# A first phase by whole batches of 512 columns in a LoRA and cross-attention kernel

## The chip, the cores and the metric

The kernel runs on one NeuronCore of a Trainium2 chip. The metric is the device time of one execution in microseconds, from the start to the end of the program on that core. In the profile, PE is TensorE (matmuls), DVE is VectorE, ACT is ScalarE, POOL is GpSimd, and SP is SyncE, whose queue only issues transfers here. All data is float32 in DRAM.

## The reference

Two layers over x of 4 batches x 512 tokens x 1024 features, with a context of 4 x 64 vectors:

```python
# layer 0: eight low-rank updates, mixed by a router
w     = softmax(einsum('bsh,nh->bsn', x, router_W) + router_b)        # 8 experts
a_sum = einsum('bsh,arh->bsr', x, ctx_4096)                           # 4 blocks of 64 rows, summed
y     = einsum('bsr,nhr->bsnh', a_sum, lora_B)
h     = nan_to_num(x + 0.5 * einsum('bsn,bsnh->bsh', w, y), nan=0, posinf=1e4, neginf=-1e4)
# layer 1: cross-attention, 32 heads of 32, 64 keys per batch, then layernorm
Q = (h @ Wq.T + bq);  K = (ctx @ Wk.T + bk);  V = (ctx @ Wv.T + bv)
attn = softmax(where(mask, Q K^T / sqrt(32), -inf))
z    = h + (attn V) @ Wo.T + bo
out  = (z - mean) / sqrt(var + 1e-5) * ln_g + ln_b
```

## The kernel before

Every large product is made in three: each float32 operand is split in a high part (rounded to the type float32r, by ACT) and a low part (the rest, by DVE), and `three` (line 499) adds high x high, high x low and low x high in PSUM. The instruction lines are L503, L504 and L505.

The first phase works on units of 256 tokens, two to a batch, eight in all. `UNIT_A` (lines 253 and 254) writes out the order in which every engine's queue goes through a unit: the logits and the low-rank sums ("route", float32 products of 72 columns), transposes of the routed rows ("expand"), eight updates ("u0" to "u7"), each the 128 rows of one chunk of h, and eight query chunks of the *previous* unit ("q0" to "q7"). While unit 0 runs, the query places hold the keys' and values' products instead ("project", KEYS_VALUES), which are float32 products without splitting. Batch 0 is written out, batches 1 to 3 are a hardware loop.

One update goes through the engines so. PE: 12 products into a bank `ps_up`. DVE: `t_sb` = 0.5 x product + x (L745), `pos` and `neg` (L750, L751), `finite` (L752). POOL: `h_t` = pos + neg (L1106). DVE: where finite, t_sb is copied over h_t (L758), which counts `h_ready`. ACT: `act_hi` = high part of h_t (L955). DVE: `act_lo` = low part (L762). PE: `h_rows` transposes h_t for the residual (L533), three chunks behind the updates, and DVE copies it out with the output bias (L770), so that it is stored as `h_rows` in DRAM. Queries are copied from PSUM by ACT (L961) and stored in DRAM whole.

The second phase is attention in 86 steps, one chunk of four heads x 256 tokens a step: scores, softmax, transposes, context, and a part of the output projection, each engine a few steps behind the other (`step` of each engine). It loads queries, keys and values from DRAM and splits them there (q: L1021 on ACT, L1119 on POOL; keys: L1004, L820; values: L1015, L829). The projection begins in step 14. The queries of the last unit stand in steps 0 to 7, and the output weights are loaded, split and put in the place of the query weights during steps 4 to 13 (`WO_SPLITS`).

SP's queue is one order for loads and stores; weights pass a ring of four `stage` tiles, and `load_weight(n)` (line 350) waits until the low part of weight n - 4 is made (`stage_lo`). All engines' queues run in the order written; an instruction that waits on a semaphore holds all behind it.

Of the kernel before, what the change touches and what calls it, by code (L numbers as in the profile page):

```python
# [13 lines left out]
P = 128  # L28
NB = 4
TOK = 512  # L30
H = 1024
KC = H // P
U = 256
UB = TOK // U
TU = U // P
CB = UB * KC
# [10 lines left out]
FAR = 3.0e38  # L47
ACT_HEADS = 4
EXPS = ACT_HEADS + 1
EPS = 1e-5  # L50
WARM = 28

REGION_3 = max(2 * KC * U + 2 * RC * U + 6 * U + 2 * U // 4, 4 * TU * HPC * V + 8 * U + 8 * U + 4 * U + 2 * KC * V)
REGION_4 = max(4 * U + 2 * NR * R + KC * LOG + 8 * P * TU + H + NR + TU * (R + 2 * NR + 3) + 64, 2 * H)


def live(i, n, per):


    return n < per and (not isinstance(i, int) or i * per + n >= 0)  # L60


def wait(eng, sem, value):

    if not isinstance(value, int) or value > 0:
        eng.wait_ge(sem, value)


def xattn_kernel(nc, xT, ctxT, mask, BT, rWT, rb, WqT, bq, WkT, bk, WvT, bv, WoT, bo, ln_g, ln_b, out):
    x_v = xT.rearrange("b (k p) t -> b p k t", p=P)  # L70
    w_v = {n: w.rearrange("(k p) n -> p k n", p=P) for n, w in
           (("q", WqT), ("k", WkT), ("v", WvT), ("o", WoT), ("B", BT))}
    ctx_v = ctxT.rearrange("(k p) v -> p k v", p=P)

    hn_d = nc.dram_tensor("h_rows", (NB, UB, U, H), F32, kind="Internal").ap()
    q_d = nc.dram_tensor("q_cols", (NB, UB, KC // 2, P, 2 * U), F32, kind="Internal").ap()

    k_d = nc.dram_tensor("keys", (NB, P, KC, V), F32, kind="Internal").ap()
    v_d = nc.dram_tensor("values", (NB * V, H), F32, kind="Internal").ap()
    k_chunks = k_d.rearrange("b p c v -> c p b v")  # L80
    v_heads = v_d.rearrange("(b v) (c s d) -> b s v c d", v=V, s=2, d=HD)
    hn_pairs = hn_d.rearrange("b u (t p) (g n) -> b u g p t n", p=P, n=2 * P)
    hn_tiles = hn_d.rearrange("b u (t p) n -> (b u t) p n", p=P)
    out_v = out.rearrange("b (t p) n -> (b t) p n", p=P)

    with ExitStack() as ctx:
        def sb(name, shape, dt=F32, stack=ctx):
            return stack.enter_context(nc.sbuf_tensor(name, shape, dt))
# [3 lines left out]

        ident = sb("ident", [P, P])
        bq_c = sb("bq_c", [P, KC])
        bk_c = sb("bk_c", [P, KC])
        bv_c = sb("bv_c", [P, KC])
        eps_c = sb("eps_c", [P, 1])
        mask_i = sb("mask_i", [P, NB * V], I32)
# [3 lines left out]

        act_hi = [sb("act_hi0", [P, KC, U], F32R)]
        act_lo = [sb("act_lo0", [P, KC, U], F32R)]
        with ExitStack() as s:
            ctx_t = sb("ctx_t", [P, KC, NB * V], F32, s)
        act_hi.append(sb("act_hi1", [P, KC, U], F32R))
        act_lo.append(sb("act_lo1", [P, KC, U], F32R))  # L110
# [12 lines left out]

        with ExitStack() as s:
            b_hi = sb("b_hi", [P, RC, H], F32R, s)
            b_lo = sb("b_lo", [P, RC, H], F32R, s)
        kbd_hi = sb("kbd_hi", [P, KC, HPC * V], F32R)
        kbd_lo = sb("kbd_lo", [P, KC, HPC * V], F32R)
        vbd_hi = sb("vbd_hi", [P, KC, 2, P], F32R)
        vbd_lo = sb("vbd_lo", [P, KC, 2, P], F32R)  # L130

        region3 = ExitStack()
        x_sb = [sb(f"x_sb{u}", [P, KC, U], F32, region3) for u in range(2)]
        u_hi = sb("u_hi", [P, RC, U], F32R, region3)
        u_lo = sb("u_lo", [P, RC, U], F32R, region3)
        t_sb = [sb(f"t_sb{k}", [P, U], F32, region3) for k in range(2)]
        pos = [sb(f"pos{k}", [P, U], F32, region3) for k in range(2)]
        neg = [sb(f"neg{k}", [P, U], F32, region3) for k in range(2)]
        finite = [sb(f"finite{k}", [P, U], U8, region3) for k in range(2)]
        region3.close()  # L140
        region3 = ExitStack()
        s_sb = [sb(f"s_sb{k}", [P, TU * HPC, V], F32, region3) for k in range(4)]
        p_hi = [sb(f"p_hi{k}", [P, 2, U], F32R, region3) for k in range(2)]
        p_lo = [sb(f"p_lo{k}", [P, 2, U], F32R, region3) for k in range(2)]
        q_hi = [sb(f"q_hi{k}", [P, U], F32R, region3) for k in range(4)]
        q_lo = [sb(f"q_lo{k}", [P, U], F32R, region3) for k in range(4)]
        q_raw = [sb(f"q_raw{k}", [P, 2, U], F32, region3) for k in range(2)]
        k_b = sb("k_b", [P, KC, V], F32, region3)
        v_b = sb("v_b", [P, KC, 2, HD], F32, region3)
        region3.close()  # L150
        sb("region3", [P, REGION_3], F32)

        region4 = ExitStack()
        h_t = [sb(f"h_t{k}", [P, U], F32, region4) for k in range(4)]
        u_sb = [sb(f"u_sb{k}", [P, NR, R], F32, region4) for k in range(2)]
        a_rhs = sb("a_rhs", [P, KC, LOG], F32, region4)
        hn_sb = [sb(f"hn_sb{k}", [P, TU, 2 * P], F32, region4) for k in range(2)]
        q_sb = [sb(f"q_sb{k}", [P, 2, U], F32, region4) for k in range(2)]
        bo_b = sb("bo_b", [P, H], F32, region4)
        rb_b = sb("rb_b", [P, NR], F32, region4)  # L160
        a_sb = sb("a_sb", [P, TU, R], F32, region4)
        lg = sb("lg", [P, TU, NR], F32, region4)
        lg_max = sb("lg_max", [P, TU], F32, region4)
        lg_sum = sb("lg_sum", [P, TU], F32, region4)
        lg_inv = sb("lg_inv", [P, TU], F32, region4)
        w_sb = sb("w_sb", [P, TU, NR], F32, region4)
        region4.close()
        with ExitStack() as s:
            g_b = sb("g_b", [P, H], F32, s)
            lb_b = sb("lb_b", [P, H], F32, s)  # L170
        sb("region4", [P, REGION_4], F32)

        with ExitStack() as s:
            stage = [sb(f"stage{k}", [P, H], F32, s) for k in range(4)]
        z_sb = [sb(f"z_sb{k}", [P, H]) for k in range(4)]
        k_sb = [sb(f"k_sb{k}", [P, NB * V]) for k in range(2)]
        v_sb = sb("v_sb", [P, H // 2])
# [3 lines left out]
        mask_b = sb("mask_b", [P, V])  # L181
# [10 lines left out]
        ps_al = ps[:, 0, 0:TU * LOG].rearrange("p (t n) -> p t n", t=TU)  # L192
        ps_u = [ps[:, 1, :], ps[:, 2, :]]
        ps_up = [ps[:, 3, 0:U], ps[:, 4, 0:U]]
        ps_hn = [ps[:, 5, 0:U], ps[:, 2, 0:U]]
        ps_q = [ps[:, 6, 0:U], ps[:, 7, 0:U]]

        ps_kv = [ps[:, 6, :], ps[:, 7, :]]
        ps_s = [ps[:, 0, :], ps[:, 1, :]]
        ps_t = [ps[:, 2, :].rearrange("p (g n) -> p g n", g=2), ps[:, 3, :].rearrange("p (g n) -> p g n", g=2)]  # L200
        ps_v = [ps[:, 4, 0:U], ps[:, 5, 0:U]]
        ps_o = [ps[:, 6, :], ps[:, 7, :]]


        ident_set, ident_ready = sem("ident_set"), sem("ident_ready")
        warm_set = sem("warm_set")
        small_in, ctx_in, router_in = sem("small_in"), sem("ctx_in"), sem("router_in")
        wk_in, wv_in = [sem(f"wk_in{g}") for g in range(KC // 2)], [sem(f"wv_in{k}") for k in range(2)]
        k_stored, v_stored = [sem(f"k_stored{k}") for k in range(2)], sem("v_stored")
        stage_in = [sem(f"stage_in{k}") for k in range(4)]  # L210
        stage_hi, stage_lo = sem("stage_hi"), sem("stage_lo")
        x_in = [sem(f"x_in{u}") for u in range(2)]
        mask_step, a_step = sem("mask_step"), sem("a_step")
        k_mm, k_out, v_mm, v_out = sem("k_mm"), sem("k_out"), sem("v_mm"), sem("v_out")
# [982 lines left out]
```

## Time and profile before

| | |
|---|---|
| median of three executions | 739.31 us (738.87 to 739.56) |
| profiled execution | 738.63 us, span of its instructions 736.8 us |
| PE busy | 698.5 us, 95% |
| DVE, ACT, POOL busy | 507.0, 323.3, 307.8 us |
| mean granted TensorE clock | 0.985 |
| moved by DMA | 76.83 MB, mean 104 GB/s |

The times of single instructions come from one profiled execution. A matmul's end is modelled and overlaps the next one's start, so that the distance from start to start is what a product costs in a row of products, not its duration. The clock is 1.00 at full speed and 0.50 at half.

### The profile page before, as it was taken

To read this page: it belongs to the slowest core of one execution; us is meant where nothing else is said; L and a number is where in the kernel's file an instruction comes from. 1 tells how busy PE (TensorE), PEld (TensorE's weight loads), DVE (VectorE), ACT (ScalarE), POOL (GpSimd) and SP (SyncE) were. 2 spreads that over 40 slices of the span, in tenths; PEclk is the share of its full clock that TensorE was granted. 3 is DMA by queue.
4 is the path that set the end of the run, shared out by engine and by line. 5 is a ranking of instruction groups with operands and counts; after the bars stand their busy time and mean duration, and the time that the engine had idled before them with its cause. 6 is when DMAs were issued, how large, how long until landed. Compare 5 with 4: busy or idle time off the path is not lost.

```text
span 736.8 us, 14456 instructions
## 1 busy us (share of the span) xinstructions
PE 698.5 (95%) x4764; PEld 638.7 (87%) x4764; DVE 507.0 (69%) x1170; ACT 323.3 (44%) x1061; POOL 307.8 (42%) x343
## 2 busy tenths in 40 slices
PE   9999999999999999999988879999998999999993
PEld 7885699999999999999978768888887888888882
DVE  2547347364745647374667898999999988998733
ACT  0412221212121222112126897777776868777511
POOL 1011022221212212221234685478667876787644
PEclk9999999999999999999999989999999999999997
DMA  8984212513130312211141462013312242222311
GB/s 280 391 294 159 85 58 75 199 44 130 44 114 28 114 57 80 77 43 71 43 115 58 141 188 88 34 51 117 102 44 87 86 117 85 86 85 72 115 58 57
DMA packets 57012, 76.83 MB, mean 104 GB/s; under 512 B 17025, under 2 KB 38657, under 8 KB 56961
## 3 DMA queue, kind: packets, MB, share of 16 engines
q1 hardware_dynamic: 56960, 76.21, 31.0%
q8 instruction: 24, 0.39, 0.2%
q14 instruction: 28, 0.22, 0.1%
HBM read 48.94 MB, written 27.26 MB: 103 GB/s over the span
## 4 chain that ended last, share of the span: by engine, by line
PE 72%; DVE 15%; issue 5%; ACT 5%; DMA 2%; POOL 0%; DVEq 0%; SPq 0%; ACTq 0%
PE ps L503 19%; PE ps L505 19%; PE ps L504 19%; PE ps L606 4%; PE ps L514 3%; PE ps L593 2%; DVE kbd_lo L820 2%; DVE s_sb L842 2%; PE ps L635 2%; PE ps L533 2%; DVE p_lo L859 2%; DVE vbd_lo L829 1%; ACT s_sb L1029 1%; PE ps L568 1%; DMA keys<-k_sb 1%
## 5 line engine op out<-in xcount | busy, mean ns | idle before, releaser
L503 PE MATMUL ps<-act_hi,w_hi 128*128 128x256 f32 x512 | 149.6, 292 | 0.6 <-issue 0.6
L505 PE MATMUL ps<-act_hi,w_lo 128*128 128x256 f32 x512 | 146.2, 286 | 0.0
L504 PE MATMUL ps<-act_lo,w_hi 128*128 128x256 f32 x512 | 146.1, 285 | 0.0
L1106 POOL TENSOR_TENSOR h_t<-pos,neg 128x256 f32<-128x256 f32 x64 | 48.3, 754 | 233.1 <-DVE neg L751 233.1
L503 PE MATMUL ps<-w_hi,act_hi 128*128 128x512 f32 x256 | 105.3, 411 | 4.1 <-DVE act_lo L864 4.1
L955 ACT ACTIVATE act_hi<-h_t 128x256 fp32r<-128x256 f32 x64 | 26.7, 417 | 174.7 <-DVE h_t L758 174.7
L505 PE MATMUL ps<-w_hi,act_lo 128*128 128x512 f32 x256 | 100.4, 392 | 0.0
L504 PE MATMUL ps<-w_lo,act_hi 128*128 128x512 f32 x256 | 100.2, 391 | 0.0
L503 PEld LDWEIGHTS ps<-act_hi,w_hi 128*128 128x128 f32 x512 | 99.4, 194 | 0.8 <-issue 0.8
L1029 ACT ACTIVATE s_sb<-s_sb,s_min 128x64 f32<-128x64 f32 x256 | 85.8, 339 | 31.8 <-DVE s_min L847 31.2
L504 PEld LDWEIGHTS ps<-act_lo,w_hi 128*128 128x128 f32 x512 | 99.4, 194 | 0.0
L505 PEld LDWEIGHTS ps<-act_hi,w_lo 128*128 128x128 f32 x512 | 99.3, 194 | 0.0
L745 DVE SCALAR_TENSOR_TENSOR t_sb<-ps,x_sb 128x256 f32<-128x256 f32 x64 | 26.9, 420 | 81.1 <-PE ps L505 81.0
L1124 POOL TENSOR_TENSOR s_sb<-s_sb,s_inv 128x512 f32<-128x512 f32 x64 | 73.7, 1152 | 16.5 <-DVE s_inv L855 16.4
L503 PE MATMUL ps<-u_hi,b_hi 128*128 128x256 f32 x256 | 74.7, 292 | 0.6 <-DVE u_lo L735 0.6
L505 PE MATMUL ps<-u_hi,b_lo 128*128 128x256 f32 x256 | 72.4, 283 | 0.0
L504 PE MATMUL ps<-u_lo,b_hi 128*128 128x256 f32 x256 | 72.4, 283 | 0.0
L1119 POOL TENSOR_TENSOR q_lo<-q_raw,q_hi 128x256 fp32r<-128x256 f32 x64 | 49.1, 768 | 48.9 <-ACT q_hi L1021 48.8
L503 PEld LDWEIGHTS ps<-w_hi,act_hi 128*128 128x128 f32 x256 | 48.5, 189 | 13.0 <-DVE act_lo L864 4.8
L505 PEld LDWEIGHTS ps<-w_hi,act_lo 128*128 128x128 f32 x256 | 48.2, 188 | 10.8
L961 ACT ACTIVATE q_sb<-ps,bq_c 128x256 f32<-128x256 f32 x64 | 30.0, 469 | 61.0 <-PE ps L505 60.4
L504 PEld LDWEIGHTS ps<-w_lo,act_hi 128*128 128x128 f32 x256 | 48.5, 189 | 8.4
(105 smaller groups left out, 1731.1 us busy)
## 6 DMA issues: line engine op xcount, KB each, us to landing
x_sb<-xT SPq DMA_DIRECT2D x8, 1024.0 KB, 6.0
h_rows<-hn_sb SPq DMA_DIRECT2D x32, 256.0 KB, 2.2
q_cols<-q_sb SPq DMA_DIRECT2D x32, 256.0 KB, 2.1
q_raw<-q_cols SPq DMA_DIRECT2D x32, 256.0 KB, 3.2
z_sb<-h_rows SPq DMA_DIRECT2D x16, 512.0 KB, 3.5
out<-z_sb SPq DMA_DIRECT2D x16, 512.0 KB, 2.9
wk_raw<-WkT SPq DMA_DIRECT2D x8, 512.0 KB, 8.4
wv_raw<-WvT SPq DMA_DIRECT2D x2, 2048.0 KB, 11.4
```

What stands on the lines that cost most here:

```text
L503: pe.matmul(dst, lh, rh, start=(first and j == 0), stop=False)
L504: pe.matmul(dst, lh, rl, start=False, stop=False)
L505: mm = pe.matmul(dst, ll, rh, start=False, stop=(last and j == n - 1))
L514: mm = pe.matmul(ps_al[:, t, :], x_sb[p][:, k, t * P:(t + 1) * P], a_rhs[:, k, :], start=(k == 0), stop=(k == KC - 1))
L606: mm = pe.matmul(ps_kv[n % 2], ctx_t[:, k, t * P:(t + 1) * P], wv_raw[k // HK][:, k % HK, half * (H // 2):(half + 1) * (H // 2)], start=(k ...
L745: dve.scalar_tensor_tensor(t_sb[c % 2][:], ps_up[c % 2], LORA_SCALE, x_sb[u][:, c, :], ALU.mult, ALU.add).then_inc(t_ready, 1)
L955: act.activation(act_hi[m // KC][:, m % KC, :], h_t[m % 4][:], ACT.Copy).then_inc(hhi_done, 1)
L961: act.activation(q_sb[c // 2 % 2][:, c % 2, :], ps_q[c % 2], ACT.Identity, bias=bq_c[:, c:c + 1]).then_inc(q_copied, 1)
L1029: act.activation(s_sb[m % 4][:, h, :], s_sb[m % 4][:, h, :], ACT.Exp, bias=s_min[m % 2][:, h:h + 1], scale=-1.0, accum_out=s_sum[m % 2][:, ...
L1106: pool.tensor_tensor(h_t[m % 4][:], pos[m % 2][:], neg[m % 2][:], ALU.add).then_inc(sign_ready, 1)
L1119: pool.tensor_tensor(q_lo[m % 4][:], q_raw[m % KC // 2 % 2][:, m % 2, :], q_hi[m % 4][:], ALU.subtract).then_inc(qlo_done, 1)
L1124: pool.tensor_tensor(s_sb[m % 4][:], s_sb[m % 4][:], s_inv[m % 2][:].unsqueeze(2).to_broadcast([P, TU * HPC, V]), ALU.mult).then_inc(p_rea ...
```

## The change

The first phase works on whole batches of 512 tokens. Query, update, key and value products all have 512 columns. The order of all engines is written by two functions, without hardware loops. Keys and values are split products as well (context rows stationary, weight rows moving), accumulated over the eight weight rows in four PSUM banks `ps_q`, and so are the queries: a "query" block is one k of the sum for four chunks, 12 products. Queries, keys, values and output weights are split in the first phase and both parts are kept in DRAM, so that the second phase only loads them. Keys are turned by PE ("turn") before they are stored. The transposes of h stand one chunk behind the updates (three before). The update's sum is made in place in `x_sb`, and `h_t` has three tiles of 512 columns. The last 12 query blocks stand in steps 0 to 11 of the second phase. The core of the diff:

```diff
+SEQ = ([("K", k) for k in range(5)] + [("B", k) for k in range(RC)] + [("K", k) for k in range(5, KC)]
+       + [("V", k) for k in range(KC)] + [("Q", k) for k in (0, 1, 3, 4, 5, 6, 7, 2)])
+def first_phase():
+    def up(i, c):
+        return ([("rows", i, c - 1)] if c else []) + [("update", i, c)]
+    out = [("context_in", 0)] + split("K", 0) + [("context_in", 1)] + split("K", 1) + [("keys", 0)] + split("K", 2)
+    out += [("adapter",), ("keys", 1)] + split("K", 3) + [("keys", 2)] + split("K", 4) + [("keys", 3), ("route", 0)]
+    out += split("B", 0, 1) + [("keys", 4)] + split("B", 2, 3) + split("K", 5) + [("keys", 5)] + split("K", 6)
+    out += [("expand", 0, 0), ("keys", 6)] + split("K", 7) + [("expand", 0, 1), ("keys", 7), ("keys_out",)]
+    out += up(0, 0) + split("V", 0) + [("values", 0)] + split("V", 1) + [("mask",), ("values", 1)] + split("V", 2) + up(0, 1)
+    out += [("values", 2), ("turn", 0), ("turn", 1)] + split("V", 3) + [("values", 3)] + split("V", 4) + up(0, 2)
+    out += [("values", 4), ("turn", 2), ("turn", 3)] + split("V", 5) + up(0, 3) + [("values", 5)] + split("V", 6)
+    out += [("values", 6)] + split("V", 7) + up(0, 4) + split("Q", 0) + [("values", 7), ("values_out",)] + split("Q", 1)
+    for i in range(NB):
+        ks = (0, 1, 3, 4, 5, 6, 7, 2) if i == 0 else range(KC)
+        for n, k in enumerate(ks):
+            out += query(i, 0, k)
+            if i == 0 and n < 6:
+                out += split("Q", ks[n + 2])
+            if n in (0, 1):
+                out += up(i, 5 + n)
+            if n == (2 if i == 0 else 3):
+                out += up(i, 7)
+                if i == NB - 1:
+                    return out
+            if n == 4:
+                out += [("rows", i, 7), ("flush", i)]
+            if i in (1, 2) and n >= 4:
+                out += [("output_weight", 8 * (i - 1) + 2 * (n - 4) + h) for h in range(2)]
+        out += [("query_out", i, 0), ("route", i + 1)]
+        for k in range(KC):
+            out += query(i, 1, k)
+            if k in (1, 2):
+                out += [("expand", i + 1, k - 1)]
+            if k == 7:
+                out += [("query_out", i, 1)]
+            if k >= 3:
+                out += up(i + 1, k - 3)
@@ the queue of SP @@
+            def load_weight(n):
+                what, k = SEQ[n]
+                wait(sp, stage_lo, n - 3)
+                sp.dma_start(stage[n % 4][:], w_v[what][k]).then_inc(stage_in[n % 4], 16)
+            def output_weight(n):
...
+                sp.wait_ge(wolo_done, n + 1)
+                for l in range(2):
+                    sp.dma_start(o_d[l, n // 2, :, n % 2 * HALF:(n % 2 + 1) * HALF],
+                                 wo_sb[:, l, :].bitcast(F32)).then_inc(wo_stored, 16)
+                if n + 2 < 2 * KC:
+                    load_raw(n + 2)
+                if n == 2 * KC - 1:
+                    sp.wait_ge(wo_stored, 32 * 2 * KC)
@@ the queue of PE @@
+            def h_rows(i, c):
+                m = KC * i + c
+                pe.wait_ge(h_ready, m + 1)
+                wait(pe, hn_copied, m)
+                for t in range(TT):
+                    mm = pe.transpose(ps_hn[:, t * P:(t + 1) * P], h_t[m % 3][:, t * P:(t + 1) * P], ident[:])
+                mm.then_inc(hn_mm, 1)
...
+            def query(i, g, k):
...
+                if g == 0:
+                    pe.wait_ge(hlo_done, KC * i + k + 1)
+                for j in range(4):
+                    if first:
+                        if i == 0 and g == 0:
+                            pe.wait_ge(kvlo_done, 4 + j + 1)
+                        else:
+                            pe.wait_ge(q_copied, KC * i + 4 * g + j - 3)
+                    cols = slice((4 * g + j) * P, (4 * g + j + 1) * P)
+                    mm = three(ps_q[j], [(w_hi[:, k, cols], w_lo[:, k, cols], act_hi[:, k, :], act_lo[:, k, :])],
+                               first=first, last=last)
+                    if last:
+                        mm.then_inc(q_mm, 1)
+                if not last:
+                    mm.then_inc(block_mm, 1)
@@ the queue of DVE @@
+            def update(i, c):
+                m = KC * i + c
+                t_c = x_sb[:, c, :]
+                dve.wait_ge(up_mm, m + 1)
+                dve.scalar_tensor_tensor(t_c, ps_up[c % 2], LORA_SCALE, t_c, ALU.mult, ALU.add).then_inc(t_ready, 1)
+                wait(dve, sign_ready, m - 1)
+                wait(dve, h_ready, m - 1)
+                dve.wait_ge(t_ready, m + 1)
+                dve.tensor_scalar(pos[m % 2][:], t_c, 0.0, 1e4, ALU.is_gt, ALU.mult).then_inc(sign_step, 1)
+                dve.tensor_scalar(neg[m % 2][:], t_c, 0.0, -1e4, ALU.is_lt, ALU.mult).then_inc(sign_step, 1)
+                if c:
+                    h_low(m - 1)
+                dve.tensor_scalar(finite[m % 2][:], t_c, 0.0, 0.0, ALU.mult, ALU.is_equal).then_inc(f_ready, 1)
+                if c:
+                    copy_h_rows(m - 1)
+                dve.wait_ge(f_ready, m + 1)
+                dve.wait_ge(sign_ready, m + 1)
+                dve.copy_predicated(h_t[m % 3][:], finite[m % 2][:], t_c).then_inc(h_ready, 1)
@@ the queue of ACT @@
+            def update(i, c):
+                m = KC * i + c
+                act.wait_ge(h_ready, m + 1)
+                if i >= 1 and c < KC - 1:
+                    act.wait_ge(block_mm, 14 * (i - 1) + 7 + c + 1)
+                if i >= 1 and c == KC - 1:
+                    act.wait_ge(q_mm, KC * i)
+                act.activation(act_hi[:, c, :], h_t[m % 3][:], ACT.Copy).then_inc(hhi_done, 1)
...
+            def output_weight(n):
+                act.wait_ge(wo_raw_in[n % 2], 16 * (n // 2 + 1))
+                wait(act, wo_stored, 32 * n)
+                act.activation(wo_sb[:, 0, :], wo_raw[n % 2][:], ACT.Copy).then_inc(wohi_done, 1)
```

Left out of the diff here: the tiles' new addresses, `turn` and `values_out` (ACT makes the high part of a bank into one of two tiles `kv_sb`, DVE the low part, SP stores both; a tile is used again when its stores have landed), the loads of q, k, v parts in the second phase, and the steps of attention, whose products and order stay.

## Rows read from the trace of the kernel before

**Rows 1.** The page, busy time by engine: us, share of the span, instructions.
```profile
PE 698.5 (95%) x4764; PEld 638.7 (87%) x4764; DVE 507.0 (69%) x1170; ACT 323.3 (44%) x1061; POOL 307.8 (42%) x343
```
**Rows 2.** Stages on all engines: length, busy us (count) by engine, clock, DMA share, GB/s.
```profile
85.07:374.80 289.73, 286.17 (x2410) 284.61 (x2408) 167.55 (x456) 59.91 (x134) 57.16 (x71) 1.00 0.23 80
374.80:439.74 64.94, 50.72 (x365) 48.21 (x363) 51.85 (x96) 48.13 (x172) 38.11 (x39) 0.91 0.43 131
439.74:703.00 263.26, 256.77 (x1529) 226.62 (x1528) 235.81 (x506) 192.28 (x718) 190.36 (x208) 1.00 0.26 84
```
**Rows 3.** PE in order of time: start, us, line; transposes in a unit, and an update's end.
```profile
137.30 1.04 PE L525 MATMUL ps<-ident,u_sb 128*128 128x128 f32 x8
138.09 0.36 PE L503 MATMUL ps<-act_hi,w_hi 128*128 128x256 f32 x1
...
148.01 0.28 PE L504 MATMUL ps<-u_lo,b_hi 128*128 128x256 f32 x1
148.13 0.28 PE L505 MATMUL ps<-u_hi,b_lo 128*128 128x256 f32 x1
```
**Rows 4.** PE in order of time, output projection in the second phase, 512 columns.
```profile
442.54 0.39 PE L503 MATMUL ps<-w_hi,act_hi 128*128 128x512 f32 x1
442.76 0.39 PE L504 MATMUL ps<-w_lo,act_hi 128*128 128x512 f32 x1
```
**Rows 5.** The chain that ended last: start, us, what.
```profile
11.12 3.76 PE ps L514 x32
...
64.43 20.62 PE ps L606 x48
...
126.81 3.53 PE ps L514 x32
```
**Rows 6.** DVE in order of time, one update of 256 columns.
```profile
148.45 0.42 DVE L745 SCALAR_TENSOR_TENSOR t_sb<-ps,x_sb 128x256 f32<-128x256 f32 x1 [2.80 <-PE ps L505]
148.91 0.30 DVE L750 TENSOR_SCALAR pos<-t_sb 128x256 f32<-128x256 f32 x1
149.12 0.28 DVE L751 TENSOR_SCALAR neg<-t_sb 128x256 f32<-128x256 f32 x1
...
149.52 0.42 DVE L762 TENSOR_TENSOR act_lo<-h_t,act_hi 128x256 fp32r<-128x256 f32 x1
149.86 0.98 DVE L758 COPY_PREDICATED h_t<-finite,t_sb 128x256 f32<-128x256 uint8 x1
```
**Rows 7.** Groups by line on DVE, ACT and POOL: busy us, mean ns, idle before.
```profile
L842 DVE SCALAR_TENSOR_TENSOR s_sb<-ps,mask_b 128x512 f32<-128x512 f32 x64 | 43.7, 683 | 14.9 <-PE ps L505 13.6 <-PE ps L635 0.8
L691 DVE TENSOR_TENSOR w_lo<-stage,w_hi 128x1024 fp32r<-128x1024 f32 x16 | 19.4, 1244 | 1.5 <-ACT w_hi L939 1.5
...
L939 ACT ACTIVATE w_hi<-stage 128x1024 fp32r<-128x1024 f32 x16 | 16.2, 1047 | 15.3 <-PE ps L606 15.3
...
L1124 POOL TENSOR_TENSOR s_sb<-s_sb,s_inv 128x512 f32<-128x512 f32 x64 | 73.7, 1152 | 16.5 <-DVE s_inv L855 16.4
L1130 POOL TENSOR_TENSOR s_sb<-s_sb,s_min 128x256 f32<-128x256 f32 x64 | 41.9, 654 | 29.4 <-DVE s_min L847 29.2
```
**Rows 8.** POOL in order of time, the same update and the next.
```profile
149.62 0.91 POOL L1106 TENSOR_TENSOR h_t<-pos,neg 128x256 f32<-128x256 f32 x1 [3.41 <-DVE neg L751]
153.80 0.73 POOL L1106 TENSOR_TENSOR h_t<-pos,neg 128x256 f32<-128x256 f32 x1 [3.27 <-DVE neg L751]
```
**Rows 9.** DVE in order of time at the start: the adapter's first sum, the router's last step.
```profile
6.40 0.69 DVE L685 TENSOR_TENSOR a_rhs<-ctx_t 128x512 f32<-128x512 f32 x1 [5.00 <-DMA ctx_t<-ctxT]
...
16.47 0.17 DVE L726 TENSOR_TENSOR w_sb<-lg,lg_inv 128x16 f32<-128x16 f32 x1
```
**Rows 10.** Tiles stage and q_sb: transfers to landing, and SP's issue of the stores.
```profile
DMA to landing us min/median/max: 3.4/7.7/12.7
...
L378 SPq DMA_DIRECT2D q_cols<-q_sb x32: 332/344/1006, 96.6 to 417.4; - x32
...
DMA to landing us min/median/max: 2.0/2.1/3.9
```

More of the change, by code:

```diff
@@ L47 @@
 FAR = 3.0e38
+EPS = 1e-5
+WARM = 22
+U = 256
+TU = U // P
+UNITS = NB * TOK // U
+CHUNKS = UNITS * KC
+TILES = NB * TOK // P
+GROUPS = 2 * TILES
+STEPS = CHUNKS + 22
 ACT_HEADS = 4
 EXPS = ACT_HEADS + 1
[L50 to L60, printed above, removed]
+BASE = 6144
@@ new lines, in second_phase @@
+def second_phase():
+    last = NB - 1
+    left = {0: [("query", last, 0, 4), ("rows", last, 7), ("flush", last)], 1: [("query", last, 0, 5)],
+            2: [("query", last, 0, 6)], 3: [("query", last, 0, 7), ("query_out", last, 0)]}
+    for n in range(8):
+        pair, k = n // 4, n % 4
+        left[4 + n] = [("pair", pair, 2 * k), ("pair", pair, 2 * k + 1)] + ([("pair_out", pair)] if k == 3 else [])
+    out = []
+    for s in range(STEPS):
+        out += left.get(s, []) + [("step", s)]
+    return out
@@ L171, in xattn_kernel @@
[L171 to L177, printed above, removed]
+        rb_b = sb("rb_b", [P, NR])
+        a_sb = sb("a_sb", [P, TT, R])
+        lg = sb("lg", [P, TT, NR])
+        lg_max = sb("lg_max", [P, TT])
+        lg_sum = sb("lg_sum", [P, TT])
@@ L506, in three, with project @@
                 return mm
-            def a_and_logits(i, p):
-                wait(pe, x_in[p], 16 * (i + 1))
-                wait(pe, route, 7 * (UB * i + p))
-                for t in range(TU):
+            pe.wait_ge(warm_set, 1)
+            for n in range(WARM):
+                pe.matmul(ps_up[0], act_hi[:, 0, 0:P], act_hi[:, 0, :], start=True, stop=True)
+            def project(what, k):
+                s = slot_of(what, k)
+                pe.wait_ge(stage_lo, PLACE[what, k] + 1)
+                for g in range(4):
+                    t, cols = g // 2, slice(g % 2 * HALF, (g % 2 + 1) * HALF)
+                    if what == "V" and k == 0:
+                        pe.wait_ge(k_copied, g + 1)
+                    rows = slice(t * P, (t + 1) * P)
+                    mm = three(ps_q[g], [(ctx_hi[:, k, rows], ctx_lo[:, k, rows], w_hi[:, s, cols], w_lo[:, s, cols])],
+                               first=(k == 0), last=(k == KC - 1))
+                return mm
@@ L674, in _, with step @@
-            run_phase_b(pe, step, lambda m: query(NB - 1, KC * (UB - 1) + m))
+            def step(s):
+                if live(s - 2, CHUNKS):
+                    scores(s - 2)
+                if live(s - 5, CHUNKS):
+                    p_transposed(s - 5)
+                o, part = output_group(s)
+                if live(o, GROUPS):
+                    projection(o, part)
+                if live(s - 6, CHUNKS):
+                    context(s - 6)
+            run({"keys": keys, "values": values, "turn": turn, "route": a_and_logits, "expand": expand, "update": update,
+                 "rows": h_rows, "query": query, "pair": pair, "step": step})
@@ L1102, in signs @@
-            def signs(i, m):
-                wait(pool, sign_step, 2 * (i * CB + m) + 2)
-                wait(pool, hn_mm, i * CB + m - 3)
-                wait(pool, hlo_done, i * CB + m - 3)
-                pool.tensor_tensor(h_t[m % 4][:], pos[m % 2][:], neg[m % 2][:], ALU.add).then_inc(sign_ready, 1)
-            run_phase_a(pool, {"route": lambda i, p: None, "expand": expand, "update": signs,
-                               "query": lambda i, m: None, "flush": lambda i, p: None,
-                               "rows": lambda i, p: None, "project": lambda n: None})
@@ new lines, in signs, with update, zero @@
+            def signs(m):
+                pool.wait_ge(sign_step, 2 * m + 2)
+                wait(pool, hn_mm, m - 2)
+                wait(pool, hlo_done, m - 2)
+                pool.tensor_tensor(h_t[m % 3][:], pos[m % 2][:], neg[m % 2][:], ALU.add).then_inc(sign_ready, 1)
+            def update(i, c):
+                signs(KC * i + c)
+            def zero():
+                pool.wait_ge(up_mm, ALL)
+                for z in (kbd[0], kbd[1], vbd[0], vbd[1]):
+                    pool.memset(z[:].bitcast(F32), 0.0).then_inc(zeroed, 1)
```

1362 lines of the change are left out of this document (621 added, 741 removed).

## The prediction

> **What bounds the kernel now.** I read the busy line first: TensorE (PE) 698.5 of 736.8 us, VectorE (DVE) 507, ScalarE (ACT) 323 [rows 1]. A busy share is an average, so the table by stages comes next [rows 2]. From 85.07 to 374.80 us (seven units of 256 tokens, 41.4 us each) PE is busy 286.2 of 289.7 us: the order in which PE's queue is written decides, and there is almost no wait in it. From 374.80 to 439.74 (attention starting up beside the last eight queries) PE is busy 50.7 of 64.9 us at a mean clock of 0.91. From 439.74 to 703.00 PE has 256.8 of 263.3 us. So time is won only by taking work from PE, and anything that makes PE wait is lost in full. The profiled execution took 738.63 us, 1.8 us around its span of 736.8, and 0.7 us below the median of 739.31.
>
> **What wider matmuls are worth.** Start to start, a 256-column product takes 0.12 us [rows 3] and a 512-column one 0.228 (0.22 to 0.23, [rows 4]); two narrow ones cost 0.240. Queries and updates have 64 x 24 + 64 x 12 = 2304 narrow products, which become 1152 wide ones: 1152 x 0.012 = 14 us. Keys and values: 24 full-precision products of 512 columns took 20.62 us [rows 5], 0.86 each; split, three take 0.68, and there are 64 in keys and values together: 64 x 0.18 = 11 us. Attention needs no splitting of q, k, v any more; its steps are then bound by PE (below). That is the gain, about 35 us with the better cover at the handover. It is what the waits have to be set against. The loops written out cost nothing that a row shows, since PE has no gap at a loop's turn in [rows 2]; the zeroing of four tiles on POOL lies under the last query blocks.
>
> **The chain of one update, 512 wide.** Call S the start of an update's last product. Now DVE starts 0.32 us after it (148.13 to 148.45, [rows 3, 6]); at 512 columns the product lasts 0.11 longer [rows 4]: 0.43. The scaled sum takes 0.42 at 256 [rows 6] and an operation like it 0.68 at 512 [rows 7], 0.26 more. Pos to neg is 0.21 at 256 [rows 6]; these compare at about twice the pace, so 0.13 more, 0.34. neg ends at about 1.91, and GpSimd (POOL) starts 0.08 later, at 1.99. Its sum is 0.73 at 256 [rows 8]; the pair 0.654 and 1.152 [rows 7] gives 0.5 more for 256 columns: 1.23. But DVE's low part of the previous chunk now stands between neg and finite, starts 0.1 us ahead of POOL and takes 0.69; a short version of this is in the trace: DVE at 149.52, POOL at 149.62, and POOL takes 0.91, not 0.73 [rows 6, 8]. So POOL ends near 3.67, and the predicated copy (a clear pass from SBUF takes 0.42 at 256 [rows 6], so 0.7 here) gives h_ready at 4.5.
> PE transposes a chunk's rows right before the *next* update (three chunks later before). Where one query block (12 x 0.228 = 2.74) stands between two updates, PE is at the transposes at S + 2.97 and waits 1.54 us. Places, from the written order: up 0 to 4 of the next batch, four; rows 4, 5 and 7 of a batch, three; batch 0 has two. 2 + 4 + 3 + 4 + 3 + 4 + 3 = 23, one of them after the handover. 23 x 1.54 = 35 us. Bounds: 1.04 each if POOL isn't delayed (24 us); if finite must wait for POOL as well, all that follows it comes after 3.67 and the wait is 2.4 (55 us).
> The predicated copy that began while POOL ran (149.86) took 0.98 [rows 6]. No row has finite beside POOL, and I take it as free, like the PSUM reads. The Trainium skill (SBUF - State Buffer, section "SBUF: two separate sides") says that a DVE instruction in a two-port mode, or with two SBUF inputs, and a GpSimd one lock each other out for the whole instruction; that row agrees; if finite counts as two-port, the sum would be by 20 us and more higher, the second rival below.
>
> **The start, walked.** Context lands at 6.4 [rows 9]. ACT's high part (1.05 for 1024 columns) and DVE's low part (1.24, [rows 7]) of half the context and of K0 follow: first keys at 9.9. PE work from there to the first query: 192 products of keys and values 43.8, one route 2 x 3.53 = 7.1 [rows 5], 16 + 16 transposes 3.5 (8 take 0.79, [rows 3], and the product behind them 0.08 more), five updates 13.7, rows 1.8: 69.8. Waits in it:
> - K5 follows four B parts in a ring of four stages, and B0 is split behind the router (1.65 us, from 14.88 [rows 5] to 16.6 [rows 9]). B0's two parts follow, and K5 is asked for 3.4 us after the route ends at 27.9; landing 3.4 to 12.7, median 7.7 [rows 10], I take 5 with the queue empty; two parts 2.3. Ready at 38.3, PE free at 30.7: 7.6.
> - ACT's act_hi of an update waits for that update's h_ready, and the V parts and turns stand behind it in ACT's queue. After update 0 (DVE copies four key banks first): V0 ready at 58.4, PE free at 51: 7.4. After update 1: the two turns, one PSUM bank, and V3: 5.9. After update 2, the turns: 3.1. After update 3, V6: 4.5. Update 4, Q0, then four value groups through two buffers, each store landing in 2.1 [rows 10]: 8.0.
> Together 36.5 us (25 to 50, by the landing and by the chain). The transfers themselves are no bound: their share is 0.23 in phase one now [rows 2], and halves of q, k, v and the output weights add less than that again. First query at 9.9 + 69.8 + 36.5 = 116.2.
>
> **The output weights.** In batches 1 and 2 eight halves pass one tile wo_sb: ACT 0.6 (1.05 for twice the columns, [rows 7]), DVE 0.69, two stores issued by SyncE at 0.35 each, the second landed 2.1 later [rows 10], then ACT goes on: 4.2 with the handshakes (3.7 if the minimum landing of 2.0 and overlap hold). ACT's copy of the query group stands behind all eight, and PE needs its bank after the route. PE is there at S + 20.2 (S of update 7; queries 4 to 7 with one wait, then 7.1). ACT gets there at S + 41.3 in batch 1 (the first raw half is only asked for behind the flush), S + 36.5 in batch 2. 21 + 16 = 37 us (28 to 45).
>
> **Sum.** Rest of phase one: 52 query blocks 142.5, 27 updates 74.0, rows 11.9, three routes 21.2, expands 5.2: 254.8. With 22 waits 33.9, a Q part late in batch 0 by 1.4, and 37: phase one ends at 116.2 + 254.8 + 33.9 + 1.4 + 37 = 443.3. Handover to the first projection: 12 query blocks now cover it, four steps with 2.74 each, scores and one wait 14.4, then ten steps at 4.4 on the mean, 44 (PE's work in one with a query block is 4.6, in one without 1.9; now the fourteen take 4.6 each): 58.4 (64.9 now, [rows 2]). SyncE's 32 extra loads a batch (0.34 each at least, [rows 10]) are asked for four steps ahead and are hidden; without that cover 3 us a batch. The 56 full steps take 263.3 now, 4.70 each; PE's work in one is 24 products, 4.64 us, so 4 us go, and 297.1 - 4 = 293 remain to the end. 443.3 + 58.4 + 293 = 794.7. Eight waits of 3 us and more let the clock fall: the handover lost 0.09 x 64.9 = 5.8 us of clock in four falls [rows 2]; eight cost some 9.5 (0 to 18). Span 804, device time **806 us**, 9% slower.
>
> **Rivals.**
> - *Finite waits for POOL too.* For: it has the quick pace of pos and neg, and both of its ends are in SBUF; against: DVE's small tensor_scalars weren't delayed. 20 us at the transposes, 5 at the start, 4 clock: 835. Chance 0.28.
> - *Store round trips are cheap or overlapped*, so ACT is with the query group in time: 806 - 37 - 3 = 766. For: 15 us of cover; against: eight round trips in series. Chance 0.1.
> - *ACT's queue doesn't hold PE* (the other side): start waits and output weights are all queue order on ACT and the stage ring, 73.5 us and 9.5 of clock. Without them 806 - 83 = 723, faster. It decides where less than 15 us of them stay. For: ACT is only 44% busy [rows 1]; against: each wait is on a semaphore that the same queue reaches later. Chance 0.08.
> - *The transposes don't wait, beside it* (the change does only what it says): 690. Chance 0.03.
> - *Worse*: repeated waits keep the clock at half: above 850. Chance 0.06.
> - Forecast, 780 to 825: 0.45.
>
> **Numbers.** Range 760 to 845: it takes in the cheap round trips and the first rival, and leaves out 0.08 + 0.03 + 0.06 and a little. Within 0.2% (what these runs can tell from nothing) 0.01; faster 0.1; slower 0.89.
>
> **What would show it.** Profile after: PE's busy share well under 90%; waits "ps <- h_t" of 1.5 us on the row transposes, 20-odd times; two waits of 15 to 21 us before a query group in the middle; phase one ending near 443; no waits in attention above those of now. It is wrong if h_ready comes within 3 us of S, if the landing of small stores is hidden, or if K5 and V0 arrive before PE wants them.

## The result

The changed kernel takes 877.62 us (median of four executions, 875.64 to 880.06) against 739.25 for the kernel before: ratio 1.1894 (95% interval 1.1864 to 1.1924). The direction was forecast, the size was not: 806 was predicted, and 877.62 lies above the range's upper end of 845. The profiled execution has a span of 876.3 us and a mean clock of 0.907.

The page of the changed kernel, its busy time and its clock in 40 slices, answers to [rows 1]:

```profile
PE 718.9 (82%) x3622; PEld 605.9 (69%) x3622; DVE 497.9 (57%) x914; ACT 295.4 (34%) x891; POOL 258.7 (30%) x249
...
PEclk9887877899899689899698898899999999999998
```

PE has 1142 fewer matmuls than before and is nevertheless busy for 20 us longer. The line of the clock shows why: digits of 6 to 8 stand all over the first 26 slices. The table by stages, with the columns of [rows 2]; the borders are the first query product, the last update's last product and the first product of the output projection:

```profile
0.00:127.70 127.70, 89.68 (x386) 72.68 (x387) 64.12 (x87) 32.41 (x40) 13.79 (x16) 0.86 0.53 168
127.70:510.80 383.10, 291.47 (x1296) 236.06 (x1297) 168.83 (x265) 55.62 (x90) 54.53 (x38) 0.86 0.33 111
510.80:587.70 76.90, 60.55 (x317) 51.92 (x315) 41.71 (x80) 34.62 (x134) 27.32 (x28) 0.90 0.66 233
587.70:876.30 288.60, 277.24 (x1628) 245.23 (x1626) 223.23 (x484) 172.70 (x627) 163.04 (x167) 0.98 0.37 116
```

PE stands still for 38.0, 91.6, 16.4 and 11.4 us in the four. I take half of PE's busy time at half clock (1.2 of 2.4 GHz) as what the clock costs. Summed over the trace's records it is 11.5, 33.2, 6.4 and 1.0 us, 52.1 in all; all such sums below are made in this way. What PE waited for, in total, times and longest:

```profile
PE ps L599 <- DVE h_t L810: 48.3, 23, 2.6
PE ps L516 <- DVE q_sb L819: 41.4, 3, 22.1
PE ps L516 <- DVE w_lo L722: 25.4, 6, 7.2
PE ps L516 <- DMA qb<-q_cols: 10.9, 3, 5.4
PE ps L516 <- DVE kv_sb L739: 9.0, 2, 5.8
PE ps L553 <- DVE kv_sb L734: 7.4, 2, 3.7
```

L599 is the transposes of h, L516 the first product of `three`. The 23 waits are the 23 that were counted from the order, but they are not 1.54 us each: nineteen are 2.2, three 1.3 and one 2.6, 2.1 on the mean. One of them on PE; the last product of an update starts at S = 228.31:

```profile
228.31 0.40 PE L518 MATMUL ps<-u_hi,b_lo 128*128 128x512 f32 x1
...
231.06 0.39 PE L518 MATMUL ps<-act_hi,w_lo 128*128 128x512 f32 x1
233.64 0.66 PE L599 MATMUL ps<-ident,h_t 128*128 128x128 f32 x4 [2.19 <-DVE h_t L810]
...
234.94 0.63 PE L516 MATMUL ps<-u_hi,b_hi 128*128 128x512 f32 x1
235.37 0.63 PE L517 MATMUL ps<-u_lo,b_hi 128*128 128x512 f32 x1
```

After the wait the products stand 0.43 us apart, no longer 0.23. The same update on DVE, and then on POOL:

```profile
228.75 0.69 DVE L797 SCALAR_TENSOR_TENSOR x_sb<-ps,x_sb 128x512 f32<-128x512 f32 x1 [5.09 <-PE ps L518]
229.57 0.43 DVE L801 TENSOR_SCALAR pos<-x_sb 128x512 f32<-128x512 f32 x1
229.91 0.42 DVE L802 TENSOR_SCALAR neg<-x_sb 128x512 f32<-128x512 f32 x1
230.25 0.69 DVE L784 TENSOR_TENSOR act_lo<-h_t,act_hi 128x512 fp32r<-128x512 f32 x1
230.85 1.50 DVE L805 TENSOR_SCALAR finite<-x_sb 128x512 uint8<-128x512 f32 x1
232.28 0.68 DVE L790 TENSOR_TENSOR hn_sb<-ps,bo_b 128x512 f32<-128x512 f32 x1
232.88 0.71 DVE L810 COPY_PREDICATED h_t<-finite,x_sb 128x512 f32<-128x512 uint8 x1
```
```profile
230.41 1.66 POOL L1076 TENSOR_TENSOR h_t<-pos,neg 128x512 f32<-128x512 f32 x1 [8.28 <-DVE neg L802]
```

`finite` reads what `pos` reads, and takes 1.50 us where that takes 0.43 (its output is uint8, but it takes 0.43 as well where POOL is idle, as the last but one experiment shows): it ends at 232.35, just after POOL (232.07). So the copy of the previous rows and the predicated copy stand behind POOL's sum, and h is ready at S + 5.28, not S + 4.5.

### The profile page after: what moved, and what is told of

Same layout as the page of the kernel before. It is cut to its first block, busy times and chain, and to the rows that moved or that the text cites. A ratio compares the mean times of both kernels' runs of the same rounds, so it can differ in the third digit from the quotient of the medians.

```text
span 876.3 us, 10740 instructions
## 1 busy us (share of the span) xinstructions
PE 718.9 (82%) x3622; PEld 605.9 (69%) x3622; DVE 497.9 (57%) x914; ACT 295.4 (34%) x891; POOL 258.7 (30%) x249
## 4 chain that ended last, share of the span: by engine, by line
PE 61%; DVE 17%; DMA 8%; issue 6%; SPq 3%; ACT 3%; POOL 2%; DVEq 0%; ACTq 0%; POOLq 0%
PE ps L516 18%; PE ps L517 18%; PE ps L518 18%; DMA output_weights<-wo_sb 4%; DVE finite L805 3%; PE ps L658 3%; PE ps L599 2%; DVE h_t L810 2%; DVE x_sb L797 2%; DVE hn_sb L790 2%; DVE act_lo L784 2%; PE ps L567 2%; DMA qb<-q_cols 2%; DVE wo_sb L832 1%; DVE neg L802 1%
## 5 line engine op out<-in xcount | busy, mean ns | idle before, releaser
L516 PE MATMUL ps<-act_hi,w_hi 128*128 128x512 f32 x256 | 106.2, 415 | 52.4 <-DVE q_sb L819 41.4
L1076 POOL TENSOR_TENSOR h_t<-pos,neg 128x512 f32<-128x512 f32 x32 | 51.9, 1622 | 290.6 <-DVE neg L802 290.6
L516 PE MATMUL ps<-wo_hi,cx_hi 128*128 128x512 f32 x256 | 105.1, 411 | 0.0
L517 PE MATMUL ps<-act_lo,w_hi 128*128 128x512 f32 x256 | 104.0, 406 | 0.0
L518 PE MATMUL ps<-act_hi,w_lo 128*128 128x512 f32 x256 | 103.6, 405 | 0.0
L517 PE MATMUL ps<-wo_lo,cx_hi 128*128 128x512 f32 x256 | 100.6, 393 | 0.0
L518 PE MATMUL ps<-wo_hi,cx_lo 128*128 128x512 f32 x256 | 100.5, 393 | 0.0
L516 PEld LDWEIGHTS ps<-act_hi,w_hi 128*128 128x128 f32 x256 | 50.9, 199 | 64.9 <-DVE q_sb L819 41.9
L797 DVE SCALAR_TENSOR_TENSOR x_sb<-ps,x_sb 128x512 f32<-128x512 f32 x32 | 22.1, 692 | 125.3 <-PE ps L518 125.3
L599 PE MATMUL ps<-ident,h_t 128*128 128x128 f32 x128 | 23.7, 315 | 48.3 <-DVE h_t L810 48.3
L516 PE MATMUL ps<-u_hi,b_hi 128*128 128x512 f32 x128 | 62.5, 489 | 0.0
L517 PE MATMUL ps<-u_lo,b_hi 128*128 128x512 f32 x128 | 59.0, 461 | 0.0
L518 PE MATMUL ps<-u_hi,b_lo 128*128 128x512 f32 x128 | 58.2, 455 | 0.0
L599 PEld LDWEIGHTS ps<-ident,h_t 128*128 128x128 f32 x128 | 16.3, 157 | 59.4 <-DVE h_t L810 58.0
```

The source lines that it names most:

```text
L516: pe.matmul(dst, lh, rh, start=(first and j == 0), stop=False)
L517: pe.matmul(dst, lh, rl, start=False, stop=False)
L518: mm = pe.matmul(dst, ll, rh, start=False, stop=(last and j == n - 1))
L599: mm = pe.transpose(ps_hn[:, t * P:(t + 1) * P], h_t[m % 3][:, t * P:(t + 1) * P], ident[:])
L797: dve.scalar_tensor_tensor(t_c, ps_up[c % 2], LORA_SCALE, t_c, ALU.mult, ALU.add).then_inc(t_ready, 1)
L1076: pool.tensor_tensor(h_t[m % 3][:], pos[m % 2][:], neg[m % 2][:], ALU.add).then_inc(sign_ready, 1)
```

## The experiments

Each is the changed kernel with one edit, unless another is named. Runs without an interval are one execution; the kernel before took 736.6 to 737.3 us beside them.

**Transposes of h two updates behind.**

```diff
 def up(i, c):
-    return ([("rows", i, c - 1)] if c else []) + [("update", i, c)]
+    return ([("rows", i, c - 2)] if c >= 2 else []) + [("update", i, c)]
@@ DVE, update @@
-    if c:
-        copy_h_rows(m - 1)
+    if c >= 2:
+        copy_h_rows(m - 2)
```

> The changed kernel with PE's transposes of a chunk two updates behind instead of one (rows 6 and 7 behind queries 4 and 5). Theory (the chain of one update, 5.3 us, is longer than the one query block that stands before the transposes, and each such wait also lets the clock fall): the 23 waits for h_t of 48.3 us in sum go, and with them some 17 short stretches at half clock, 20 to 25 us: 877.6 - 48 - 22 = 807, between 800 and 815. Rival (the chain only moves its wait to the next thing that needs the chunk, the query's low part): the waits return under another name and less than 20 us go, 858 or more.

Measured: 837.93, between what was expected and the rival's time. The waits for h are gone, and another has come:

```profile
PE ps L605 <- DVE hn_sb L796: 34.9, 17, 5.2
```

The transposes have one PSUM bank, and DVE's copy out of it stands behind `finite` in DVE's update. The expected time was missed because 34.9 of the 48.3 us came back there. Yet in this run the stage from the first query to the last update lost only 10.2 us to the clock, not 33.2:

```profile
125.90:468.02 342.12, 267.94 (x1295) 220.48 (x1296) 169.29 (x265) 55.68 (x90) 54.52 (x38) 0.91 0.37 124
```

**The test of finiteness first.**

```diff
     dve.wait_ge(t_ready, m + 1)
+    dve.tensor_scalar(finite...).then_inc(f_ready, 1)
     dve.tensor_scalar(pos...)
     dve.tensor_scalar(neg...)
     if c:
         h_low(m - 1)
-    dve.tensor_scalar(finite...).then_inc(f_ready, 1)
```

> The changed kernel with the comparison finite ahead of pos instead of behind the low part. Theory (finite takes 1.50 us instead of 0.42 because it waits for POOL's sum, and the two operations behind it come late): finite is 0.42, h_ready comes 0.4 to 0.6 us earlier, 23 waits shrink from 2.2 to 1.7: 11 us and a few falls of the clock less, 855 to 866. Rival (finite is only slow beside POOL but not on the path, since the predicated copy must wait for POOL anyway): 875 to 880, or slower by the 0.34 that POOL starts later, 885.

Measured: 866.01, at the upper end of what was expected. The waits for h fall from 48.3 to 42.7 us, and the clock's loss in the stage from 33.2 to 25.4. `finite` beside POOL costs about 12 us here, of which half is the waits themselves.

**The output weights' halves spread over batches 1 and 2.**

```diff
-            if i in (1, 2) and n >= 4:
-                out += [("output_weight", 8 * (i - 1) + 2 * (n - 4) + h) for h in range(2)]
...
             out += query(i, 1, k)
+            if i in (1, 2):
+                out += [("output_weight", 8 * (i - 1) + k)]
```

> The changed kernel with the sixteen halves of the output weights one behind each query block of the second group (batches 1 and 2) instead of eight in a row ahead of the first group's copy. Theory (eight serial store round trips hold ACT's queue ahead of the query copy): the waits of 22.1 and 18.2 us for q_sb go, and 3 to 5 us of slow products behind them: 832 to 838. Rival (a round trip of 4 us holds ACT wherever it stands): waits of PE for copies, for act_hi or for u_hi come up in the second group, and less than 20 us go.

Measured: 830.79, 46.8 less, and 1 us better than was expected. The waits for the query group fall from 41.4 us to this:

```profile
PE ps L516 <- DVE q_sb L819: 2.5, 1, 2.5
```

**Work in place of the waits.** In batches 1 to 3 PE runs nine more products of 512 columns, whose result nobody reads, ahead of the transposes of h. These are 24 places, at 21 of which the changed kernel waits.

```diff
+                if i >= 1:
+                    for n in range(FILL):
+                        pe.matmul(ps_turn, w_hi[:, 1, 0:P], w_hi[:, 0, 0:HALF], start=True, stop=True)
                 pe.wait_ge(h_ready, m + 1)
```

> The changed kernel with nine extra 512-column products, whose result nothing reads, ahead of each wait for the transposes in batches 1 to 3 (21 places, 2.05 us of work at full clock each). It leaves nothing of the reference out. Theory (the clock falls because PE is idle for 2.2 us in each cycle, and a cycle takes 9.9 us where 8.3 would do): waits for h_t shrink to 0.2 us each and the clock stays at full, so that the time falls although work is added, by 20 to 30 us: 850 to 858. Rival (the cycle is set by DVE's chain, and the clock costs nothing on it): 877 or, with the added work where chain was shorter, up to 885.

Measured: 869.22, 8.4 less; 850 to 858 was expected, so the size was missed. The waits for h fall to

```profile
PE ps L603 <- DVE h_t L814: 9.1, 20, 2.2
```

and where an update follows an update with one query block between, the distance goes from 9.93 to 8.38 us although PE now does nine products more. Over the stage the clock costs 13.8 us, not 33.2. Places that had no wait, or a short one, became longer (8.7 to 10.7 us in three), and ate more than half of what the clock gave. What follows for this kernel: a standstill of 2.2 us costs itself and, in most cycles, about 1.5 us of half clock behind it; filling it gives back the second part alone.

**Copy of the rows ahead.** The first experiment, and DVE copies the transposed rows before it waits for the update's products.

```diff
             def update(i, c):
+                if c >= 2:
+                    copy_h_rows(m - 2)
                 dve.wait_ge(up_mm, m + 1)
```

> As in the run with the rows' transposes two updates behind, and VectorE's copy of a block's transposed rows stands ahead of its wait for the update's products, so that it no longer ends behind the finiteness test of the same update. If the waits for the rows and the clock that falls with them are what makes the updates slow, the 34.9 us of waits for the one PSUM bank of the rows go and the time is 795 to 810 us. Rival: VectorE's own work in an update has become the bound, so that a wait for another bank takes their place: 825 us or more.

Measured: 811.23, 26.7 below the first experiment and 66.4 below the changed kernel. The waits for the bank are 5.4 us in all. 811 is 1 us outside what was expected, far from the rival's 825. The stage from the first query to the last update is

```profile
124.73:444.02 319.29, 267.69 (x1296) 221.65 (x1296) 171.42 (x266) 55.69 (x90) 54.80 (x38) 0.90 0.39 134
```

Beside the first experiment's stage, which had sixteen waits of 1.7 to 2.7 us for the bank, PE is busy for as long (267.69 and 267.94 us), and the clock costs 11.0 us and 10.2. So those sixteen waits cost their own length and no clock that these sums can tell. What the clock still costs here stands beside the long waits, 22.6 and 17.8 us for the query group above all.

**Another order at the start.**

```diff
-    ... split("K", 4) + [("keys", 3), ("route", 0)]
-    out += split("B", 0, 1) + [("keys", 4)] + split("B", 2, 3) + split("K", 5) + [("keys", 5)] + split("K", 6)
+    ... split("K", 4) + split("B", 0, 1, 2, 3) + split("K", 5)
+    out += [("keys", 3), ("route", 0), ("keys", 4), ("keys", 5)] + split("K", 6)
...
-    out += up(0, 0) + split("V", 0) + [("values", 0)] ...
+    out += split("V", 0) + up(0, 0) + [("values", 0)] ...
@@ ACT @@
             def update(i, c):
-                (high part of h, chunk m)
+                if c:
+                    h_high(KC * i + c - 1)
```

> The changed kernel with another order at its start alone: keys' split and first turned blocks ahead of the router, the values' splits one block earlier, ScalarE's rounding of h one update behind, one turned block for each values block. If the 38 us that TensorE stands still before the first query product, with 11 us of half clock beside them, are waits for parts of the weights behind other work of VectorE and ScalarE, 835 to 848 us. Rival: the splits themselves (VectorE's time) bound this stretch, so that the waits only move: 862 us or more.

Measured: 841.86, as expected. The first query product stands at 93.3 us, not 127.7, and the stage is

```profile
0.00:93.30 93.30, 82.68 (x386) 67.23 (x387) 58.61 (x80) 32.00 (x38) 12.21 (x15) 0.96 0.72 230
```

The same 386 matmuls take 82.68 us of PE, not 89.68: 7 us of busy time are gone (the clock costs 3.4 us, not 11.5), and 27.4 of standstill.

**SyncE's queue between the phases.**

```diff
-                sp.wait_ge(zeroed, 2)
-                load_keys(0, 0)
                 sp.wait_ge(sign_ready, ALL)
                 sp.wait_ge(h_ready, ALL)
-                load_q(0)
-                load_q(1)
+                for n in range(4):
+                    load_q(n)
+                sp.wait_ge(zeroed, 2)
+                load_keys(0, 0)
@@ step s @@
-                if live(s + 1, CHUNKS) and s >= 1:
-                    load_q(s + 1)
+                if live(s + 2, CHUNKS) and s >= 2:
+                    load_q(s + 2)
```

> The changed kernel with SyncE's queue in another order between the phases: the first four blocks of queries are asked for ahead of the keys, later ones two steps ahead, the second half of the values at a later step. If the 10.9 us of waits for queries read back, and the half clock behind them, come from the loads' place in SyncE's queue, the time is 860 to 869 us. Rival: the landing of the stores or the zeroing holds them, not the queue: 873 us or more.

Measured: 867.26, as expected. From the last update to the first projection it takes 64.4 us, not 76.9, and the waits for queries read back are 0.4 us in all. One wait of 2.3 us before a scores product is left, for which the profile names no releaser. The rows that it answers to, SP's queue in the changed kernel and PE in the same time:

```profile
530.64 2.59 SPq L429 DMA_DIRECT2D vbd_hi<-values  x4
533.27 2.59 SPq L429 DMA_DIRECT2D vbd_lo<-values  x4
535.91 2.59 SPq L429 DMA_DIRECT2D vbd_hi<-values  x4
538.55 2.59 SPq L429 DMA_DIRECT2D vbd_lo<-values  x4
541.18 3.02 SPq L383 DMA_DIRECT2D q_cols<-q_sb  x4
544.30 1.12 SPq L437 DMA_DIRECT2D qb<-q_cols  x1
```
```profile
544.10 0.39 PE L518 MATMUL ps<-act_hi,w_lo 128*128 128x512 f32 x1
549.88 0.58 PE L516 MATMUL ps<-kbd_hi,qb 128*128 128x256 f32 x1 [5.39 <-DMA qb<-q_cols]
```

Sixteen loads of values hold SP for 10.5 us, 0.65 each, four stores for 3.0, and the load that PE wants next is asked for only behind them.

**All of these together** (rows two behind with their copy ahead, weights spread, start, SyncE's queue).

> All of it together: rows two updates behind with their copy ahead, the output weights' halves one behind each block of queries, the other order at the start, the other order of SyncE's queue between the phases. If each of them takes away a wait of its own, the gains add up and the time is 690 to 720 us, faster than the kernel before. Rival: behind the removed waits stands a limit of VectorE or of the clock that they hid, and the time stays over 735 us.

Measured: 714.93, ratio 0.9666 (0.9613 to 0.9719): faster than the kernel before, as expected. The single gains, 66.4 + 46.8 + 35.8 + 10.4 = 159.4, would give 718.2: they add up within the spread of the four executions (707.9 to 716.5), so each was a wait of its own. One wait of 7.6 us for the bank of the rows was left, at the end of phase one. DVE there, and POOL:

```profile
356.86 0.68 DVE L791 TENSOR_TENSOR act_lo<-h_t,act_hi 128x512 fp32r<-128x512 f32 x1
357.46 8.49 DVE L814 TENSOR_SCALAR finite<-x_sb 128x512 uint8<-128x512 f32 x1
365.98 0.73 DVE L817 COPY_PREDICATED h_t<-finite,x_sb 128x512 f32<-128x512 uint8 x1
```
```profile
357.02 1.67 POOL L1094 TENSOR_TENSOR h_t<-pos,neg 128x512 f32<-128x512 f32 x1 [3.57 <-DVE neg L811]
358.62 1.81 POOL L1102 MEMSET kbd_hi<- 128x2048 f32 x1
360.37 1.81 POOL L1102 MEMSET kbd_lo<- 128x2048 f32 x1
362.12 1.80 POOL L1102 MEMSET vbd_hi<- 128x2048 f32 x1
363.87 1.80 POOL L1102 MEMSET vbd_lo<- 128x2048 f32 x1
```

The test of finiteness came in behind five instructions of POOL that follow one another without a gap, and ended 0.3 us behind the last of them.

**All together, the test of finiteness first.**

> All the changes of the last run together, and the finiteness test of an update ahead of the tests of the sign that GpSimd waits for, so that GpSimd is idle while it runs. In the last run the test of the last update took 8.49 us, beside four zeroing instructions of GpSimd, and 7.6 us of TensorE's waits stood behind it. If a test takes long only while GpSimd works, no test is over 0.5 us except beside the router's work on GpSimd, the wait of 7.6 us goes, some half clock with it, and the time is 702 to 710 us. Rival: another wait takes its place, since the predicated copy and the rounding wait for the same GpSimd anyway: 713 us or more.

Measured: 712.08, ratio 0.9656 (0.9629 to 0.9684). That is 2 us outside what was expected and not quite at the rival's 713, but the intervals of this run and of the one before overlap, so that a gain between the two is not shown by the times. The trace shows the mechanism (the test of finiteness: shortest, median, longest, in ns; then the table of the second and third stage):

```profile
L810 DVE TENSOR_SCALAR finite<-x_sb x32: 426/427/428, 49.9 to 358.9; 128x512 uint8<-128x512 f32 x32
```
```profile
93.90:357.60 263.70, 256.90 (x1296) 214.22 (x1295) 147.53 (x272) 56.96 (x92) 57.75 (x39) 1.00 0.48 160
357.60:423.00 65.40, 56.20 (x321) 48.47 (x319) 39.92 (x79) 33.73 (x129) 26.02 (x27) 0.97 0.75 253
```

All 32 tests now take 0.43 us. The handover takes 65.4 us and not 71.9, while the start took 1.9 and the middle 0.8 longer.

**The same, rows one update behind again.**

> The same kernel, but with the rows' transposes and their copy again one update behind, as in the changed kernel. If the waits for h and the fall of the clock that comes with them cost the same whatever is done elsewhere, the difference between the changed kernel with the finiteness test first and the one with rows two behind and the copy ahead comes back: about 50 us over the kernel beside it, 755 to 770 us, which is slower than the kernel before. Rival: with all other waits gone the clock does not fall at waits of 2 us, so that only their own 23 x 1.85 = 43 us come back at most: 750 us or less.

Measured: 768.20, ratio to the kernel before 1.0424 (1.0382 to 1.0466), as expected. Where the transposes of h and their copies stand decides between 3.4% faster and 4.2% slower. The second stage of this kernel, and its waits for h:

```profile
95.20:415.60 320.40, 275.62 (x1296) 223.87 (x1296) 147.78 (x271) 58.15 (x92) 57.27 (x39) 0.95 0.39 133
```
```profile
PE ps L600 <- DVE h_t L811: 44.2, 24, 2.7
```

Beside the run before, the same 1296 matmuls: the stage is 56.7 us longer, 38.0 of it more standstill (44.8, not 6.8) and 18.7 more busy time (275.62, not 256.90), of which the records put 16.8 on the half clock. So these waits (most of them 1.86 us) pull the clock down even where next to nothing else waits; the rival, by which they would not, is out. Why they do, and the sixteen waits of the first experiment did not, no run here settles.

## Why the prediction was wrong

The forecast's sum gives a span of 804.2; the span is 876.3, 72.1 more. By its own steps:

- **The clock, the step that failed.** "Eight waits of 3 us and more let the clock fall ... eight cost some 9.5 (0 to 18)". It cost 52.1: 42.6 of the 72.1. The term was wrong in two ways.
  - It counted only the long waits. The 23 short ones let the clock fall as well: the last experiment has hardly any other wait, and loses 16.8 us in its second stage, while the kernel beside it loses none.
  - It priced the long waits too low. With the short waits gone and the long ones left (the experiment with the rows' copy ahead), the clock still costs 30.2 us, three times 9.5; only the other 22 go with the short waits. The row that it was read from (5.8 us in four falls) would already make 11.6 for eight.

  In the changed kernel the 1296 matmuls of the second stage take 291.47 us, and 256.90 where the clock does not fall: 34.6 more, of which the records put 33.2 on the half clock. The forecast had the rival "repeated waits keep the clock at half: above 850", with a chance of 0.06. The time is above 850 and repeated waits did it, but the clock did not stay at half: it fell and rose again, and was at half for 104 of the stage's 383 us.
- **finite as free.** "No row has finite beside POOL, and I take it as free." It is held until POOL has done, 1.50 for 0.43. POOL itself went as forecast (1.66 against 1.23 and 0.45 of delay). The waits are 2.1 us on the mean in place of 1.54, 48.3 in all for 35. The mechanism is that of the rival "Finite waits for POOL too", which had 2.4 and a chance of 0.28; its 835 was still short of the clock. Shown by the tests' 0.43 us when they stand ahead of POOL's work, and by 11.6 us less in time.
- **The start.** The eight waits were named one by one and are 38.3 us for 36.5 (K5 7.2 for 7.6, V0 6.7 for 7.4, V6 5.1 for 4.5, the values 9.0 for 8.0, the turns and V3 10.3 for 9.0). The first query block ends at 136.6, forecast 118.9: 14.3 of the 17.7 are half clock, already in the first point.
- **The output weights.** 22.1 and 18.2 us for 21 and 16. Right.
- **The rest of phase one** (from there to 510.8): 374.2 us for 324.4. Of the 49.8 more, 30.4 are clock, 16.0 longer waits (12.2 for h, 3.3 for the output weights, 0.5 for a Q part), and the remaining 3.4 were not traced.
- **The handover.** 76.9 for 58.4. 6.4 are clock and 10.9 the three waits for queries read back. The step was "SyncE's 32 extra loads a batch (0.34 each at least, [rows 10]) are asked for four steps ahead and are hidden". They take 0.44 to 0.82 us each of SP, and what they hold is not themselves but the queries' load behind them. The experiment on SyncE's queue takes these waits away, all but 0.4 us.
- **Attention.** 288.6 us for 293: the gain of phase two was 8.5 us and not 4.

Of the gain that was reckoned, "about 35 us", most is seen once the waits are out: that kernel is 25.1 us faster than the one before (737.17 to 712.08), with PE busy for 672.2 us and not 698.5, and with 27 us of standstill left ahead of the projection. In the changed kernel 165.5 us of waits and their clock (877.62 to 712.08) stood on top of it. That the whole 35 us is there is not shown.

The Trainium skill (SBUF — State Buffer, section "SBUF: two separate sides") says that a DVE instruction in a two-port mode and one of GpSimd exclude each other for the whole instruction. The trace agrees: 1.50 us beside POOL's sum, 8.49 beside the zeroing, 0.43 alone. The same section says that two SBUF inputs conflict only with a GpSimd instruction that reads SBUF. What these traces show fits: the predicated copy, two inputs, takes 0.71 at 515.30 us in the changed kernel while POOL zeroes, and 0.98 for half the columns beside POOL's sum in [rows 6].

## What to carry to other kernels

Price a standstill of TensorE by more than its length: here 23 waits were 48 us by themselves, and with nothing else waiting some 17 us of half clock came on top of 44. It is not a fixed price: sixteen waits of 1.7 to 2.7 us in another order cost no clock that could be told, so read it from the granted clock of the stage. A wait that recurs on PE is worth taking out of the order, by letting the consumer come one step later, before anything is made wider. When a stage is made coarser, each chain of the other engines grows with the tile while the work that covers it keeps its place: recount where every consumer stands. Put DVE's tests from SBUF to SBUF where POOL is idle, and in SyncE's queue count small loads by their issue time and put what PE wants next ahead of them.

## What the hardware showed beyond expectation

- A DVE instruction can be held behind a whole row of POOL instructions: 8.49 us for a test of 0.43, behind a sum and four zeroings. In the changed kernel, where the same two met at 513.28 us, the test got in between POOL's sum and the first zeroing (1.50 us), and that zeroing took 2.08 us, not 1.80. Which of the two gets in was not settled.
- Filling the standstill with products that nobody reads made update cycles with more work in them shorter, 8.38 for 9.93 us.
- SP's issue of a load of values took 0.65 us and of keys 0.44 to 0.82 in the changed kernel, where a store of queries took 0.33 in the kernel before [rows 10].
